# Five graph layers on one core: gathering node rows in groups while the last chunk still runs, and carries through a table by node

## The reference

```python
def _pna_layer(x, src, dst, edge_attr, eW, eb, pW, pb, poW, pob, lW, lb):
    ee = edge_attr @ eW + eb
    h = jnp.concatenate([xt[dst], xt[src], ee_b], axis=-1)
    h = jnp.einsum('etk,tkf->etf', h, pW) + pb
    ssum = jax.ops.segment_sum(h, dst, num_segments=n)
    cnt = jax.ops.segment_sum(jnp.ones(...), dst, num_segments=n)
    mean = ssum / jnp.maximum(cnt, 1.0)[:, None, None]
    mx = jax.ops.segment_max(h, dst, num_segments=n)
    out = jnp.concatenate([xt, mean, ssum, mx], axis=-1)
    out = jnp.einsum('ntk,tkf->ntf', out, poW) + pob
    return jax.nn.relu(out.reshape(n, T * FT) @ lW + lb)
...
for l in range(L):
    x = _pna_layer(x, src, dst, edge_attr, edge_W[l], ...)
```

## Time and profile before

| | |
|---|---|
| median of 3 runs | 11489.69 us (11487.98 to 11491.17) |
| span of the profiled execution | 11493.4 us |
| busy in that span | PE 10456.3, DVE 8163.2, ACT 6663.2, POOL 8130.8 us |
| last five layers | 5348.8 us (first scan) to the end |
| from one layer's fix row (line 1040) to the next's | 6453.15, 7694.65, 8933.06, 10171.70, 11409.5: some 1239 us |

### The profile page before, as it was taken

How to read it: one execution, slowest core, us unless ns; L and a number is a source line. 1 busy time by engine, 2 the same in 40 slices (tenths; PEclk the granted TensorE clock), 3 DMA queues, 4 the chain that set the end, 5 groups by cost and what they waited for, 6 DMA issues and landing times. The chain is left out here.

```text
span 11493.4 us, 152259 instructions
## 1 busy us (share of the span) xinstructions
PE 10456.3 (91%) x55143; PEld 9959.3 (87%) x55143; DVE 8163.2 (71%) x11101; ACT 6663.2 (58%) x6595; POOL 8130.8 (71%) x8260
## 2 busy tenths in 40 slices
PE   4999759996999999998999799979999799979997
PEld 4999758885999999998999799979999799979996
DVE  5767658886888888886666566656666566656665
ACT  2444335555888888884555455545555455535554
POOL 3777777775666666664777677767777677767776
PEclk9999979997999999999999899989999899989998
DMA  6333234434333333332333233323333233323332
GB/s 215 118 120 106 80 74 98 100 98 126 90 84 85 88 85 87 86 85 76 107 107 108 76 111 110 109 85 100 111 107 107 78 107 110 111 75 107 110 107 78
DMA packets 657979, 1157.05 MB, mean 101 GB/s; under 512 B 187206, under 2 KB 446019, under 8 KB 638787
## 3 DMA queue, kind: packets, MB, share of 16 engines
q1 hardware_dynamic: 353303, 819.43, 21.5%
q0 software_dynamic: 288992, 294.48, 12.7%
q10 hardware_dynamic: 15384, 40.39, 1.1%
HBM read 776.79 MB, written 419.18 MB: 104 GB/s over the span
## 5 line engine op out<-in xcount | busy, mean ns | idle before, releaser
L2240 PE MATMUL ps<-qs,oh 128*128 128x416 f32 (+1 forms) x26880 | 5291.9, 352 | 129.6 <-ACT oh L2330 59.9
L2119 POOL DMA_INDIRECT l3g<-TQ,srcs x4480 | 4306.1, 961 | 1524.6 <-issue 1079.8
L2240 PEld LDWEIGHTS ps<-qs,oh 128*128 128x128 f32 x26880 | 4867.5, 188 | 400.2 <-DVE l3g L2411 214.2
L2411 DVE TENSOR_REDUCE l3g<-ps 128x32 f32<-128x416 f32 x3360 | 1894.5, 583 | 1563.2 <-PE ps L2240 1563.0
L2330 ACT CAST oh<-nd 128x1536 fp32r<-128x1536 bf16 x1120 | 1654.9, 1478 | 1692.3 <-DVE nd L2407 1692.3
L1989 PE MATMUL ps<-l2mm,l2oh 128*128 128x408 f32 (+1 forms) x12544 | 2391.3, 352 | 24.4 <-DVE l2mm L2061 24.4
L1989 PEld LDWEIGHTS ps<-l2mm,l2oh 128*128 128x128 f32 x12544 | 2333.5, 189 | 65.0 <-DVE l2mm L2061 25.2
L1973 POOL DMA_INDIRECT l2g<-Y,place x1568 | 1598.2, 1019 | 816.6 <-DVE l2mm L2061 400.0
L2061 DVE TENSOR_TENSOR l2mm<-l2hl,psv 128x1768 fp32r<-128x1768 f32 x784 | 1532.2, 1992 | 262.6 <-PE ps L1989 258.7
L2004 ACT ACTIVATE l2oh<-l2far,l2one 128x512 fp32r<-128x512 f16 x1568 | 1135.2, 724 | 294.0 <-PE ps L1989 291.5
L1151 POOL DMA_INDIRECT l0g<-T,srcs x896 | 968.7, 1081 | 420.0 <-issue 224.2
(11 more groups left out here) (394 smaller groups left out, 7303.8 us busy)
## 6 DMA issues: line engine op xcount, KB each, us to landing
W<-l3o SPq DMA_DIRECT2D x140, 1792.0 KB
mneg<-KG SPq DMA_DIRECT2D x280, 384.0 KB
l3km<-KG SPq DMA_DIRECT2D x280, 360.0 KB
l3g<-TQ,srcs POOLq DMA_INDIRECT x4480
l3t<-AT SPq DMA_DIRECT2D x140, 448.0 KB, 3.9
W<-l1o SPq DMA_DIRECT2D x28, 952.0 KB, 4.1
l0e<-U_a SPq DMA_DIRECT2D x28, 896.0 KB, 4.6
S<-RX SPq DMA_DIRECT2D x49, 512.0 KB
```

What stands on the lines that cost most here:

```text
L2119: e.indirect_dma_start(G3[s][:, j, :], None, TQ, bass.IndirectOffsetOnAxis(ap=srcs[:, c * C + j:c * C + j + 1], axis=0)).then_inc(z3[f"g{s ...
L2240: x_ = e.matmul(ps[k % 3][:, 0:32 * n], OH[k // SB][:, g, 128 * (k % SB):128 * (k % SB) + 128], QS[:, p, 32 * n0:32 * (n0 + n)], start=g = ...
L2411: e.tensor_reduce(G3[r // KP % 3][:, C - KP + r % KP, :], ps[r % KP % 3][:, 0:32 * PH].rearrange("p (h f) -> p f h", f=32), AXX, ALU.max). ...
```

## The change

The change touches the last chunk of each layer, what follows it, and some preparation ahead of the layers:

- The last chunk of a layer takes 32 picks (`KPE`) and 24 gathers in place of 24 and 32. A third, 8 picks wide, one-hot block goes with it. The order of blocks, keys and buffers is renumbered (`blocks3`, `block3`, `picked3`).
- Node rows are gathered group by group in the order 2, 3, 1, 4, 0, 5, 6 (`ORD`). Each group waits only until the chunks that it needs are stored (`s_stored`, against `needi`, which `needs_v` and `needs_t` work out once from `lastq`). With the inputs of the reference the table comes out as 28, 13, 16, 20, 24, 28 and 28 chunks for the groups 0 to 6.
- The carries no longer go into `W3`. `carries_t` and `carries_v` turn them out of the scan's last column, POOL scatters them into a table by node, `TF`, before its fourth group, and SP loads the whole of `TF` into `O3[1]` (semaphore `s_fx`). `z` adds them there: two more VectorE instructions for each group.
- Once, in layer 0, SP fills `TF` and the last chunk's part of `W3` with a neutral row. `carry_rows_v` and a third small load prepare the indices.

```diff
+KPX = 8
+KPE = KP + KPX
+ORD = (2, 3, 1, 4, 0, 5, 6)
+BEFORE_FIX = 3
...
+                if c == 2:
+                    e.wait_ge(s_neutral, 1)
+                    e.dma_start(TF[0:NP, :].rearrange("(p c) f -> p c f", p=128),
+                                neutral[:, None, :].to_broadcast([128, NC, 64])).then_inc(s_neutral, 16)
+                    e.dma_start(slots(W3, (NCH - 1) * C, C), neutral[:, None, :].to_broadcast([128, C, 64])).then_inc(s_neutral, 16)
...
         def layer3_g(e):
+            def node_rows(l, g):
+                e.wait_ge(s_stored, need[g] + NCH * l)
+                e.sem_inc(s_begun, 1)
+                for c in range(GR * g, GR * g + GR):
+                    e.indirect_dma_start(O3[0][:, c, :], None, W3,
+                                         bass.IndirectOffsetOnAxis(ap=lastq[:, c:c + 1], axis=0)).then_inc(ngs[g], 16)
...
-                    for j in range(C - KP):
+                    for j in range(C - picks3(i)):
...
                 e.wait_ge(*z3.at("o0", 16 * (l + 1) * NCH // 2))
-                e.wait_ge(*z3.at("o1", 16 * (l + 1) * NCH // 2))
-                fix_g_row(e, F3, W3, 64, feq, 1 + l)
-                fix_g_back(e, F3, W3, 64, feq, 1 + l)
-                node_gather_g(e, O3[0][:, 0:NC, :], W3, lastq)
+                for q, g in enumerate(ORD):
+                    if q == BEFORE_FIX:
+                        e.wait_ge(f_["new"], 2 + l)
+                        e.indirect_dma_start(TF, bass.IndirectOffsetOnAxis(ap=fixn[:, 0:1], axis=0), FR3,
+                                             None).then_inc(f_["back"], 16)
+                    node_rows(l, g)
...
+            def landed(i):
+                e.wait_ge(*z3.at(f"o{i % 2}", 16 * (i // 2 + 1)))
+                e.sem_inc(s_stored, 1)
+
             def store(i):
+                if i % NCH:
+                    landed(i - 1)
                 e.wait_ge(*z3.at("lay", 2 * i + 2))
...
-                    for b in range(NB3):
-                        if NB3 * i + b + 2 < NB3 * ALL3:
-                            keys(NB3 * i + b + 2)
+                    for m in range(blocks3(i) + 2, blocks3(i + 1) + 2):
+                        if m < blocks3(ALL3):
+                            keys(m)
                     if c:
                         store(i - 1)
                 store(l * NCH + NCH - 1)
+                landed(l * NCH + NCH - 1)
+                e.wait_ge(f_["back"], 16 * (2 + l))
+                e.dma_start(O3[1][:, 0:NC, :], TF[0:NP, :].rearrange("(p c) f -> p c f", p=128)).then_inc(s_fx, 16)
...
                 for step in range(2):
                     lay(i, step)
+                for step in range(2):
                     if l < 4:
                         masks(i + 1, step)
...
+                e.wait_ge(s_fx, 16 * (l + 1))
+                e.wait_ge(vec, a)
+                a = vc.up(e.tensor_tensor(nd[:, c0:c1, :], nd[:, c0:c1, :], Fx[:, c0:c1, 0:32], ALU.add).then_inc(vec, 1))
                 e.wait_ge(ngs[g], 16 * GR * (3 + l))
-                b = vc.up(e.tensor_tensor(nd2[:, c0:c1, :], PN[:, c0:c1, :], Zb[:, c0:c1, 32:64],
+                b = vc.up(e.tensor_tensor(nd2[:, c0:c1, :], Fx[:, c0:c1, 32:64], Zb[:, c0:c1, 32:64],
+                                          ALU.max).then_inc(vec, 1))
+                e.wait_ge(vec, b)
+                b = vc.up(e.tensor_tensor(nd2[:, c0:c1, :], PN[:, c0:c1, :], nd2[:, c0:c1, :],
                                           ALU.add).then_inc(vec, 1))
```

More of the change, by code:

```diff
@@ L76, in paced, with picks3, picked3, blocks3 @@
     return picks * j // (C - picks) - AHEAD
+def picks3(i):
+    return KPE if i % NCH == NCH - 1 else KP
+def picked3(i):
+    return KP * i + KPX * (i // NCH)
+def blocks3(i):
+    return NB3 * i + i // NCH
+def block3(m):
+    l, r = divmod(m, NB3 * NCH + 1)
+    c = min(r // NB3, NCH - 1)
+    return l * NCH + c, r - NB3 * c
+def gathered3(i):
+    return sum(C - picks3(k) for k in range(i % 3, i + 1, 3))
 class Chain:
@@ L491, in attributes_s @@
         def attributes_s(e):
-            e.wait_ge(od["keys"], 32)
+            e.wait_ge(od["keys"], 48)
             e.wait_ge(s_srcs, 16)
@@ L1794, in layer1_v @@
             weights3_v(e, vc)
+            needs_v(e, vc)
+            e.wait_ge(s_need, 5)
             weights2_v(e, vc)
@@ L1854, in weights3_t, with needs_v, floor, needs_t @@
                          start=True, stop=True).then_inc(w3["mm"], 1)
+        def needs_v(e, vc):
+            x_, whole, over, part = (st[:, i, :] for i in range(4))
+            def floor(by, to, tmp):
+                a = vc.up(e.tensor_scalar(x_, x_, 1.0 / by, 0.5 / by, ALU.mult, ALU.add).then_inc(vec, 1))
+                e.wait_ge(vec, a)
+                a = vc.up(e.tensor_copy(nodei[:, :], x_).then_inc(vec, 1))
+                e.wait_ge(vec, a)
+                a = vc.up(e.tensor_copy(to, nodei[:, :]).then_inc(vec, 1))
+                e.wait_ge(vec, a)
+                a = vc.up(e.tensor_tensor(tmp, to, x_, ALU.is_gt).then_inc(vec, 1))
+                e.wait_ge(vec, a)
+                a = vc.up(e.tensor_tensor(to, to, tmp, ALU.subtract).then_inc(vec, 1))
+                e.wait_ge(vec, a)
+            a = vc.up(e.tensor_copy(x_, lastq[:, :]).then_inc(vec, 1))
+            e.wait_ge(vec, a)
+            floor(C, whole, over)
+            a = vc.up(e.tensor_copy(x_, whole).then_inc(vec, 1))
+            e.wait_ge(vec, a)
+            floor(NCH, over, part)
+            a = vc.up(e.scalar_tensor_tensor(out=whole, in0=over, scalar=-float(NCH), in1=whole, op0=ALU.mult,
+                                             op1=ALU.add).then_inc(vec, 1))
+            e.wait_ge(vec, a)
+            e.tensor_reduce(part[:, 0:NGR], whole.rearrange("p (g c) -> p g c", c=GR), AXX, ALU.max).then_inc(s_need, 1)
+            e.wait_ge(s_need, 2)
+            a = vc.up(e.tensor_reduce(x_[0:NGR, 0:1], ps[4][0:NGR, 0:128], AXX, ALU.max).then_inc(vec, 1))
+            e.wait_ge(vec, a)
+            e.tensor_scalar(x_[0:NGR, 1:2], x_[0:NGR, 0:1], 1.0, None, ALU.add).then_inc(s_need, 1)
+            e.wait_ge(s_need, 4)
+            e.tensor_copy(needi[:, :], ps[4][0:1, 128:128 + NGR]).then_inc(s_need, 1)
+        def needs_t(e):
+            e.wait_ge(s_need, 1)
+            e.transpose(ps[4][0:NGR, 0:128], st[:, 3, 0:NGR], ident[:, :]).then_inc(s_need, 1)
+            e.wait_ge(s_need, 3)
+            e.matmul(ps[4][0:1, 128:128 + NGR], st[0:NGR, 0, 1:2], ident[0:NGR, 0:NGR], start=True,
+                     stop=True).then_inc(s_need, 1)
         def weights3_v(e, vc):
@@ L2108, in layer3_g @@
         def layer3_g(e):
+            def node_rows(l, g):
[4 more added lines that the diff above has]
+                                         bass.IndirectOffsetOnAxis(ap=lastq[:, c:c + 1], axis=0)).then_inc(ngs[g], 16)
+            e.wait_ge(s_need, 5)
+            need = [e.value_load(needi[0:1, g:g + 1], min_val=1, max_val=NCH) for g in range(NGR)]
+            e.wait_ge(s_neutral, 33)
             for l in range(5):
@@ L2261, in layer3_t @@
                 e.wait_ge(*z3.at("parts", PARTS3 * (l + 1)))
-                with nc.Fori(l * NCH, (l + 1) * NCH, engines=[e.engine], hint_back_edge=True,
+                with nc.Fori(l * NCH, (l + 1) * NCH - 1, engines=[e.engine], hint_back_edge=True,
                              head_slot={e.engine: 0}) as i:
                     for k in range(KP):
-                        pick(i, k)
+                        pick(l, i, k)
                         if k in MIX:
@@ L2268, in layer3_t @@
                 i = (l + 1) * NCH
-                e.wait_ge(*z3.at("lay", 2 * i))
+                for k in range(KPE):
+                    pick(l, i - 1, k)
+                    if k in MIX:
+                        mix(l, i - 1, MIX.index(k))
                 e.wait_ge(*z3.at("eev", 4 * i))
-                fix_t(e, F3, O3[(i - 1) % 2][:, C - 1, :], 64, 1 + l)
-                e.wait_ge(*z3.at("red", KP * i))
+                e.wait_ge(*z3.at("red", picked3(i)))
+                carries_t(e, l)
                 if l < 4:
@@ L2503, in layer3_v @@
                     i = l * NCH + c
-                    for k in range(KP):
-                        r = KP * i + k
-                        take(r)
-                        one_hots(r // SB + 1, SPREAD[k % SB])
+                    for k in range(picks3(i)):
+                        take(i, k)
+                        one_hots(blocks3(i) + k // SB + 1, SPREAD[k % SB] if k < KP else SPREADX[k % SB])
                         if c and k in (2, 4):
```

169 lines of the change are left out of this document (123 added, 46 removed).

## The result

| | before | after |
|---|---|---|
| median of 4 runs | 11488.83 us (11486.91 to 11491.17) | 11378.63 us (11371.59 to 11385.12) |
| span of the profiled execution | 11493.4 us | 11383.4 us |

The ratio is 0.9904, with a 95% interval of 0.989 to 0.9918: 110 us faster, against a forecast of 11390 and a range of 11362 to 11430.

A forecast was written before the change was run, and what follows sets the result against it. POOL's node gathers were taken to bound each layer's end, then the chain of groups. -4 x 23.1 - 18 + 2 + 1.5 + 7 = -100 from 11493.4 gives 11393.4; median 3.7 lower, 11390, range 11362 to 11430.

The forecast's parts named there:

- The last chunk: End of a layer's chunks: eight more picks make the adds wait until 6436.9 in place of 6432.2, +4.7 us.
- Chunk 26's store and POOL's gap: Before the node gathers: store moves from 6412.5 to 6421.6, lands at 6428; POOL stands idle from 6421 to 6428.
- The scatter and the table: Ahead of the groups: scatter lands at 6456.8; table load from 6457.9 takes 6.6 us; first group's z goes on at 6464.5.
- The chain of groups: Seven groups after the table: third multiply ends at 6483.3, seventh at 6507.3 against 6530.35, -23 us a layer.
- P: Time for each of the last four groups in the chain: between 5.2 and 6.4 us, taken as 6.0.
- One reading behind P: TensorE in the groups: the multiply took 1.65 us instead of 3.04 where work ahead of it stood without a gap.
- "The chain of groups then decides": End of a layer: last rows at about 6492, 30.6 us earlier, but TensorE's and VectorE's group work sets the end.
- a sign of being wrong: Last groups: VectorE waiting for node rows would show that POOL is still the bound.
- the chain keeps up with POOL: Rival, groups at P of 4.6: -30.6 us in four layers, -24 in the fifth, -135 in all, 11355; 8%.
- The fifth layer: Layer norm instead of products: groups 7.15 us each, VectorE's, ending at 6515.6 in place of 6534.0, -18 us.
- The set-apart halves: Halves of the set-apart nodes now come last: +0.5 us in each of four layers, +2.
- The fill: Layer 0: 13,440 neutral rows into TF and W3 take 49 us and delay a key load, +7 us, 0 to 30 likely.

The follow-up runs named there:

- x0: Changed kernel with 24 picks and 32 gathers in the last chunk, as in the kernel before: 11389.76 us, ratio 0.9911.
- fix2: Changed kernel with the scatter ahead of the third group instead of the fourth: 11383.73 us, ratio 0.9908.
- x0_fix2: Changed kernel with 24 picks in the last chunk and the scatter ahead of the third group: 11383.83 us, ratio 0.9907.
- split: Changed kernel with the table by node read back in three loads, the first two groups' columns first: 11377.59 us, ratio 0.9902.
- keys_late: Changed kernel with chunk 26's store issued ahead of the last chunk's last key load, not behind it: 11373.81 us, ratio 0.9899.
- the set that won: best_a with 4 further picks in the last chunk in place of 8: 11363.06 us, ratio 0.9883.
- warm: Changed kernel with 50 identity transposes on TensorE ahead of the turning of the carries and 110 behind it, each layer: 11374.38 us, ratio 0.9904.
- best_warm: best_a with 65, 38 and 90 identity transposes on TensorE around and in `carries_t`: 11393.04 us, ratio 0.9907.
- best_a: Changed kernel with chunk 26's store ahead of the last key load, group 0 ahead of group 4, table in three loads: 11369.86 us, ratio 0.9889.
- best_c: best_a with 4 further picks in place of 8 and the scatter ahead of the third group, on another chip: 13916.36 us, ratio 0.9922.

## Why the prediction was right

**The last chunk:** right. First add at 6440.16 - 3.2 = 6437.0, forecast 6436.9; +4.7 us on VectorE's line. Its worth is another matter: the forecast gave the picks no value, and x0 shows none.

**Chunk 26's store and POOL's gap:** right in place, 2.6 us short in size. Issued at 6424.59 - 3.2 = 6421.4 (forecast 6421.6; its own terms give 6421.4), but the first node row came 9.2 us behind the issue, not 6.4. SP takes note of the landing 8.4 us behind the issue, and POOL's gather stands 0.8 behind that. The four transfers of keys issued just ahead are what differs: in the fifth layer, which has none there, the same store had landed after 6.2 us, and in x0, whose last keys go 10.5 us ahead, after 6.0 to 6.3 in its first four layers.

**The scatter and the table:** the load took 6.6, as taken. The scatter came 2.7 us late with the first row, and Z at 6469.17 - 3.2 = 6466.0 instead of 6464.5.

**The chain of groups:** right in total, less so on the way. The third multiply ended at 6487.64 - 3.2 = 6484.4 (forecast 6483.3), the seventh at 6508.04 - 3.2 = 6504.8 (forecast 6507.3): -25.5 us against -23. P was not one number: 6.3 us from the second to the fifth `mixed`, at 1.2 GHz, then 5.0 and 2.9. In the other layers it is 4.9 to 5.2 once the clock is up. Here two errors offset each other: P was below 6.0 in the last two groups and above it in the two ahead of them, so the nearness of the total is in part luck. The Trainium skill's rule (TensorE: Matmul & The Clock Gate, Part 1) is that sustained activity releases the throttled clock. The trace does not follow it in this layer: TensorE is 93% busy at the lower level for three intervals of 6.3 us. One reading behind P does not hold either: ahead of the group whose multiply took 1.65 us, the timeline before has a gap of 2.4 us, and ahead of the one that took 3.04 a gap of 3.7, so "without a gap" does not tell the two apart.

**"The chain of groups then decides":** the step that was weakest. The last rows were forecast to be there at 6492, 30.6 us earlier than before, and so out of play. But a last row has a way of its own to the end, which the forecast never added. Before, the last multiply ended 7.7 us behind the first use of the last rows (6522.66 to 6530.35). That makes 6499.7, 7.6 us under the forecast's chain. The rows were 3 us later (6495.90 - 3.2 + 2.5 = 6495.2), for the most part through the longer gap, and the chain 2.5 us faster. That left them 2 to 4 us apart in the first layer; in the second VectorE waited 1.7 us for the last rows, which the forecast had named as a sign of being wrong, and in the third and fourth they came with at most 2 us to spare. The forecast's rival "the chain keeps up with POOL" was, then, nearly true, at a later time of POOL's than it had.

**The fifth layer:** forecast -18, measured -16.8, the groups 7.0 to 7.4 apart but for the last, 5.2 (forecast 7.15).

**The set-apart halves:** from the end of the seventh multiply to the next layer 8.5 us, and 7.9 before: +0.6, forecast +0.5.

**The fill:** forecast +7, measured 0. The chunk spacing of layer 0 did not change, and SP's queue shows why (after):

```profile
250.10 1.17 SPq L1262 DMA_DIRECT2D TF<-RX  x1
251.32 9.23 SPq L1264 DMA_DIRECT2D W<-RX  x1
280.04 0.32 SPq L1249 DMA_DIRECT2D W<-l0e  x1
```

The issue of the second fill took 9.2 us, but the queue had no work until 280, and the load of keys was there in time. All one-off parts together: the first scan of the layers at 5352.86 against 5348.8, forecast +8.5. In the twelve traces taken at the usual speed it varies from 5342.9 to 5359.1, so 4 us is not told from nothing.

**In sum:** -108.4 forecast for the five layers, -113.4 measured; +8.5 and +4.1 ahead of them. Both differences go the same way and are under 6 us each; 11390 less the two is 11380.6, and the median is 11378.6.

## What to carry to other kernels

When a long serial stage is overlapped, add to each of its parallel lines its own way to the end, and compare the lines: here the gathers were dismissed by their last row, without the 8 to 11 us behind it. Where two lines end within a microsecond or two, an edit that moves one pays little (fix2, x0_fix2 and split moved Z by 2.6 to 5.1 us and won nothing in the table; keys_late moved the rows by 7.1 and Z by 2.0 and won 2.8), and edits have to be tried in sets: the set that won moved both. Ask each time whether the engine at the meeting point waits, and for what; the distance alone varies with the clock. Before reordering a queue, look again at what each waiting instruction in it stands before once everything else has become faster.

## What was not expected of the hardware

Beside a TensorE that turned the identity, some large transfers took longer: the table's load 7.9 to 8.1 us instead of 6.4 to 6.7 in warm's first four layers, and chunk 27's store with its landing 7.6 to 8.0 instead of 5.7 (best_warm against best_a). But it isn't the turning alone: in warm's fifth layer the load took 6.6 with the transposes running all through it, and in three of its first four layers chunk 27's store took 6.0 to 6.2. The cause stays open.

The granted clock was 0.98 in a window of 5 us in which TensorE did almost nothing, and 0.50 from the next instruction on. That was behind 4.4 us without work, and behind 4.7 in best_warm. In warm's fifth layer it stood for only 1.84 us, and the first turning ran at the upper level:

```profile
11317.50 0.98 PE L2380 MATMUL ps<-ident,l3g 128*128 128x128 f32 x7 [1.84 <-DVE l3g L2650]
```

The next was at the lower one again (1.74 us), so the clock kept up to the start did not last. No run here kept TensorE at work right up to the first group of the other layers.

On the chip of best_c the same kernel before took 14025 us instead of 11490, with a mean granted clock of 0.902 to 0.908 against 0.955 to 0.961 on the others. Only one chip did so; why is open.
